# Experts on the chosen tokens alone: routing lists on chip, gathered rows, one-hot sums

## The chip, the cores and the metric

The kernel runs on one core of a Trainium2 chip. The metric is the device time in microseconds (us). A core has TensorE (PE, matrix products), VectorE (DVE), ScalarE (ACT), GpSimd (POOL) and SyncE (SP); each runs its own list of instructions in order, and they wait for each other through semaphores. TensorE first loads a stationary matrix (shown apart, as PEld) and then streams the moving one. Results of TensorE lie in PSUM, eight banks of 128 x 512 f32; everything else lies in SBUF, of 128 partitions.

## The reference

The input is x, 2 batches of 1024 tokens of 128 numbers. Four layers are added to it one after the other, each on a layer norm of x: attention A (16 heads, rotary part), the expert layer, attention B, and the same expert layer again. The case is about the expert layer:

```python
capacity = max(1, int(Sz * CAP_FACTOR / E) + 1)        # 257 for 1024 tokens, 8 experts
scores = softmax(einsum('bsd,ed->bse', x, router_w))
gate_vals, sel_idx = top_k(swapaxes(scores, 1, 2), capacity)
tokens = x[b_idx, sel_idx]                             # (2, 8, 257, 128)
h = gelu(einsum('becd,edh->bech', tokens, w1) + b1)    # 128 -> 512
y = einsum('bech,ehd->becd', h, w2) + b2               # 512 -> 128
out = zeros_like(x).at[b_idx, sel_idx].add(y * gate_vals[..., None])
```

Each expert takes the 257 tokens of a batch that score highest for it. A token can be taken by several experts, or by none.

## The kernel before

The program runs the stages attention A, expert layer 1 (`k` = 0), attention B, expert layer 2 (`k` = 1). Between two stages all engines meet (`nc.Block`). An expert layer is `feed_forward_stage` (L1207). The change leaves the attention stages alone, but for where one of their buffers is allocated.

**Head of the stage.** The tokens are in four chunks of 512. Of each chunk `turn` (L1305) turns the normalised rows by TensorE, so that the 128 numbers of a token lie in the partitions; ScalarE copies them from PSUM twice, as the rounded high part `xr[0]` (L1410) and as `xt` in full (L1411); VectorE makes the low part `xr[1]`, what the rounding left (`split`, L1456). `logits` (L1313) are products of `xt` and the router. Short products without use (`keep_busy`, L417) stand between these steps. After the last logits VectorE and ScalarE make the softmax (L1514 to L1519).

**Main loop.** The experts run over all tokens, not over the chosen ones: 8 experts x 4 chunks = 32 rounds `q`. `hidden` (L1344) is four groups of three products with 512 moving columns (high x high, high x low, low x high part); ScalarE applies the gelu (L1437) and rounds the result (L1443), VectorE makes its low part (`low`, L1461). `output` (L1357) is again twelve such products, one round later. So a round has 24 products of 512 columns, a stage 768. `gate` (L1466) multiplies the output by the gate, which is zero where the token wasn't chosen, and adds it up; at the end `turn_sum` (L1338) turns the four sums back and `finish` (L1488) adds them to x.

**Routing inside the loop.** Which tokens are chosen is found by a search for the 257th largest score of each expert, bit by bit, 30 steps (`step`, L1534): VectorE counts the scores at or above a trial value (L1526), one small product adds the counts over the tiles (L1328), VectorE sets the bit. These steps stand at fixed places (`FIRST_COUNT`, `COUNT_EVERY`) between the groups of products of the first rounds. Nothing in the products depends on them: the first three experts' outputs are kept (`ykeep`, L1446) and gated after the search. The gates go to DRAM and come back spread over the partitions, by SP's queue (L1266). The weights of an expert come through the same queue, two experts ahead (L1257).

**What sets the order.** `vector_events`, `load_events` and `routing` write out by hand at which place (`u`) of the loop each small step stands; TensorE, ScalarE and VectorE follow that list.

Of the kernel before, what the change touches and what calls it, by code (L numbers as in the profile page):

```python
# [13 lines left out]
ALU = mybir.AluOpType  # L14
# [7 lines left out]
P = 128  # L22
# [118 lines left out]
KEEP = 3  # L141
CHUNKS = NE * NCH
BITS = range(29, -1, -1)
SCORE_TURN, FIRST_COUNT, COUNT_EVERY = 4, 6, 3
TIES = FIRST_COUNT + len(BITS) * COUNT_EVERY
NGS = 8


def unit_of(q):

    return 8 * q - 4 if q else 0


def beside_step(u):

    return u + (FIRST_COUNT - u) % COUNT_EVERY if u < TIES else u


def vector_events():

    events = []
    for q in range(CHUNKS):
        events.append((beside_step(unit_of(q) + 5), 1, "low", (q, 0, 2)))
        events.append((beside_step(unit_of(q) + 8) if q else 8, 1, "low", (q, 2, 4)))
        if q >= KEEP * NCH:
            events.append((unit_of(q) + 17, 2, "gate", q))
        else:
            events.append((unit_of(q + KEEP * NCH + 3) + 11, 3, "gate", q))
        if q >= CHUNKS - NCH:
            events.append((unit_of(q) + 24, 4, "finish", q - CHUNKS + NCH))  # L170
    for i in range(len(BITS)):
        events.append((FIRST_COUNT + i * COUNT_EVERY, 0, "step", i))
    events.append((TIES, 0, "ties", 0))
    return sorted(events, key=lambda event: event[0:2])


def load_events():

    events = [(0, 0, "first", 0), (0, 1, "second", 0), (0, 2, "first", 1), (0, 3, "second", 1), (TIES, 4, "gates", 0)]
    for e in range(2, NE):  # L180
        events.append((unit_of((e - 1) * NCH) - 3, 5, "first", e))
        events.append((TIES if e == KEEP + 1 else unit_of((e - 1) * NCH) + 14, 6, "second", e))
    at = [u for u, _, what, q in EVENTS if what == "gate"]
    for n in range(CHUNKS):
        events.append((TIES if n < NGS else at[n - NGS] + 1, 7, "spread", n))
    return sorted(events, key=lambda event: event[0:2])


EVENTS = vector_events()
GATED = [q for _, _, what, q in EVENTS if what == "gate"]  # L190
LOADS = load_events()
LOWS = [q for _, _, what, q in EVENTS if what == "low"]
LOW_DONE = {(q, first): n + 1 for n, (q, first, end) in enumerate(LOWS)}

# [65 lines left out]
def constants(nc, ctx, m, a):  # L260
# [4 lines left out]
    with ExitStack() as local:  # L265
# [4 lines left out]
        b2 = sb("b2_rows", [NE, D], F32)  # L270
        small = local.enter_context(nc.psum_tensor("c_turn", [P, CH], F32))
        with nc.Block() as block:

            @block.sync
            def _(sp):
# [8 lines left out]
                sp.wait_ge(loaded, 16 * (NCH + 4))  # L284
# [28 lines left out]
            @block.tensor  # L313
            def _(pe):
                pe.wait_ge(loaded, 16 * (NCH + 4))
                pe.wait_ge(made, 6)
                pe.transpose(small[:, 0:NE], rw[:, :], m.ident[0:NE, 0:NE]).then_inc(turned, 1)
                pe.transpose(small[:, P:P + NE * HB], b1[:, :], m.ident[0:NE * HB, 0:NE * HB]).then_inc(turned, 1)
                pe.transpose(small[:, 2 * P:2 * P + NE], b2[:, :], m.ident[0:NE, 0:NE]).then_inc(turned, 1)

            @block.vector
            def _(dve):
                dve.wait_ge(loaded, 16 * (NCH + 4))
                dve.tensor_copy(m.peers[:, :, :], peers[:, :, :])
                dve.wait_ge(turned, 3)
# [87 lines left out]
IDLE = {"project": {"a": 0, "b": 36}, "attend": {"a": 34, "b": 10}, "piece": 2, "sum": 8, "turn": [(0, 0, 10, 0), (4, 4, 22, 0)],  # L413
# [754 lines left out]
def project_and_attend(nc, ctx, m, a, kind, norm):  # L1168

    loaded = [ctx.enter_context(nc.semaphore(f"loaded_{kind}{i}")) for i in range(NBUF if kind == "a" else WAYS)]  # L1170
    with ExitStack() as local:
        sb = lambda name, shape, dt: local.enter_context(nc.sbuf_tensor(f"{kind}_{name}", shape, dt))
        shape, count = ([P, GH, T], NBUF) if kind == "a" else ([P, GH // 2, T], WAYS)
        m.q2, m.k2 = [[sb(f"{side}2_{i}", shape, F32R) for i in range(count)] for side in "qk"]
# [4 lines left out]
        with nc.Block() as block:  # L1179
# [27 lines left out]
def feed_forward_stage(nc, ctx, m, a, k, sb, banks, out, norm):  # L1207

    sem = lambda name: ctx.enter_context(nc.semaphore(f"f{k}_{name}"))
# [5 lines left out]
    turned, x_taken, x_split = sem("turned"), sem("x_taken"), sem("x_split")  # L1215
    logits_ready, exp_done, scored = sem("logits_ready"), sem("exp_done"), sem("scored")
    rows_turned, count_ready, total_ready = sem("rows_turned"), sem("count_ready"), sem("total_ready")
    h_mm, gelu_done, h_high, h_low = sem("h_mm"), sem("gelu_done"), sem("h_high"), sem("h_low")
    y_mm, kept, gated = sem("y_mm"), sem("kept"), sem("gated")
    gates_out, sum_ready, sum_turned, finished = sem("gates_out"), sem("sum_ready"), sem("sum_turned"), sem("finished")  # L1220

    peak, e_x, total, score = sb("peak", [P, NT]), sb("e", [P, NT, NE]), sb("total", [P, NT]), sb("score", [P, NT, NE])
    rows = sb("rows", [P, P])
    trial, drop = sb("trial", [P, 1], I32), sb("drop", [P, 1], I32)
    above, count, totals = sb("above", [P, P]), sb("count", [P, 2], BF16), sb("totals", [P, 2])
    tied, rank, need, take = sb("tied", [P, P]), sb("rank", [P, P]), sb("need", [P, 1]), sb("take", [P, P])
    gate_rows = sb("gate_rows", [P, P])
    xr = [sb(f"xr_{i}", [P, B * T], F32R) for i in range(2)]
    w1r, w2r = [[sb(f"w{w}r_{i}", [P, 2, HID], F32R) for i in range(2)] for w in (1, 2)]
    h = [sb(f"h_{i}", [P, HB, CH]) for i in range(2)]  # L1230
    hr = [[sb(f"hr_{i}_{j}", [P, HB, CH], F32R) for j in range(2)] for i in range(2)]
    ykeep = sb("ykeep", [P, KEEP * NCH, CH])
    scaled = [sb(f"scaled_{i}", [P, CH]) for i in range(2)]
    total_t = m.xn[:, :, :].rearrange("p t d -> p (t d)")
    spread = [t[:, i * CH:(i + 1) * CH] for t in (m.v[:, :, :].rearrange("p t d -> p (t d)"), m.xt[:, :]) for i in range(NCH)]

    h_ps, y_ps = banks[:, 0:HB, :], banks[:, HB:HB + 2, :]
# [3 lines left out]
    t_ps = [banks[:, 6 + c % 2, :] for c in range(NCH)]
    use = {q: n for n, q in enumerate(GATED)}
    weights_in = lambda e: 16 * (k * NE // 2 + e // 2 + 1)
    gates_in = lambda n: 16 * (k * CHUNKS // 2 + n // 2 + 1)
# [445 lines left out]
```

## Time and profile before

| | us |
|---|---|
| three runs: lowest, median, highest | 1047.78, 1048.47, 1049.33 |
| profiled execution: span, first to last instruction | 1043.1 |
| median minus that span | 5.4 |
| expert layer 1: first expert product to end of stage | 349.8 to 539.5 |
| expert layer 2: first expert product to last work of TensorE and VectorE | 853.7 to 1040.4 |
| TensorE, VectorE, ScalarE busy of the span | 91%, 71%, 66% |
| granted TensorE clock, mean | 0.981 |

The page gives the span of the profiled execution, and no time of its own beside it; the 5.4 us are what lies before and after. The page reads as follows: part 1 is busy time by engine, part 2 the span in 40 slices (with the granted TensorE clock and the DMA share), part 4 the chain of waits from the last instruction back, part 5 the costliest groups. In a group, "128x512 f32 x768 | 191.4, 397" means 768 instructions that write 128 partitions by 512 numbers, 191.4 us busy in all, 397 ns each; "128\*128" ahead of it is the size of the stationary matrix. Matmuls overlap, so the distance from start to start, not the duration of one, says how fast they go.

### The profile page before, as it was taken

What the parts mean: (1) busy time and instruction counts of PE and PEld (TensorE: products, weight loads), DVE (VectorE), ACT (ScalarE), POOL (GpSimd) and SP (SyncE); (2) the same over time, 40 slices, a digit from 0 to 9 for tenths busy, and PEclk for the clock granted to TensorE, in tenths of its full rate; (3) what the DMA queues carried; (4) which work ended last, traced back from release to release, by engine and by line L of the source; (5) the groups of instructions that cost most, each with busy time, mean ns of one, the idle gap of its engine ahead of it and who ended that gap; (6) DMA issues with size and microseconds to landing.
All of it is one profiled execution on the core that took longest, in us unless ns stands there. A gap on an engine that the chain in (4) does not pass through costs nothing. (4 is left out here: it accounts for less than half of the span.)

```text
span 1043.1 us, 16038 instructions
## 1 busy us (share of the span) xinstructions
PE 950.8 (91%) x5690; PEld 617.5 (59%) x5690; DVE 743.1 (71%) x1318; ACT 691.1 (66%) x1180; POOL 219.0 (21%) x494
## 2 busy tenths in 40 slices
PE   3879999999998899999987899999999889999997
PEld 2545555665655677888764344444444367778886
DVE  4786776677644667699875877777777457678996
ACT  2425666666665698888734356666666759898885
POOL 1352355563333000000005113222332200000000
PEclk9999999999999899999999699999999999999999
DMA  3752442213111011355505360111000021115542
GB/s 91 208 174 41 145 115 74 56 63 91 63 42 45 38 41 41 88 136 141 121 3 131 81 184 1 32 32 32 2 2 1 2 81 41 41 62 125 141 150 51
DMA packets 67727, 78.52 MB, mean 75 GB/s; under 512 B 6512, under 2 KB 55552, under 8 KB 67264
## 3 DMA queue, kind: packets, MB, share of 16 engines
q1 hardware_dynamic: 62432, 72.83, 25.2%
q10 hardware_dynamic: 5216, 4.66, 1.6%
q8 instruction: 46, 0.75, 0.3%
q14 instruction: 33, 0.27, 0.1%
HBM read 53.44 MB, written 22.94 MB: 73 GB/s over the span
## 5 line engine op out<-in xcount | busy, mean ns | idle before, releaser
L1062 ACT ACTIVATE b_pt<-b_banks 128x512 f32<-128x512 f32 (+1 forms) x320 | 154.8, 558 | 99.1 <-PE b_banks L976 98.9
L1369 PE MATMUL f_banks<-f_hr,f_w2r 128*128 128x512 f32 x768 | 189.1, 394 | 3.6 <-DVE f_hr L1463 2.5
L1353 PE MATMUL f_banks<-f_xr,f_w1r 128*128 128x512 f32 x768 | 191.4, 397 | 0.7 <-ACT f_h L1437 0.7
L1437 ACT ACTIVATE f_h<-f_banks,b_t 128x512 f32<-128x512 f32 x256 | 167.2, 682 | 32.3 <-PE f_banks L1353 29.8
L1463 DVE TENSOR_TENSOR f_hr<-f_h,f_hr 128x1024 fp32r<-128x1024 f32 x128 | 156.1, 1223 | 28.1 <-ACT f_hr L1443 26.1
L1369 PEld LDWEIGHTS f_banks<-f_hr,f_w2r 128*128 128x128 f32 x768 | 141.7, 188 | 32.3 <-issue 3.4
L1353 PEld LDWEIGHTS f_banks<-f_xr,f_w1r 128*128 128x128 f32 x768 | 143.3, 191 | 29.6 <-ACT f_h L1437 1.5
L1085 DVE TENSOR_REDUCE a_mlate<-a_banks 128x2 f32<-128x1024 f32 (+3 forms) x120 | 124.7, 1079 | 49.8 <-PE a_banks L914 31.1
L1085 DVE TENSOR_REDUCE b_mlate<-b_banks 128x2 f32<-128x1024 f32 (+3 forms) x120 | 125.7, 1080 | 36.1 <-PE b_banks L924 18.0
L1443 ACT ACTIVATE f_hr<-f_h 128x1024 fp32r<-128x1024 f32 x128 | 136.0, 1063 | 4.1
L1062 ACT ACTIVATE a_q_hl<-a_banks 128x512 f32<-128x512 f32 (+1 forms) x160 | 81.8, 557 | 65.0 <-PE a_banks L976 63.5
L976 PE MATMUL a_banks<-a_q,a_k 121*128 121x512 f32 (+3 forms) x384 | 117.1, 383 | 3.6 <-DMA a_q<-a_mt 2.6
L1062 ACT ACTIVATE a_k_hl<-a_banks 128x512 f32<-128x512 f32 (+1 forms) x160 | 82.2, 557 | 53.4 <-PE a_banks L976 51.8
L914 PE MATMUL a_banks<-a_k,a_q 120*128 120x512 f32 (+3 forms) x384 | 99.2, 361 | 11.3 <-DVE a_mlate L1085 7.7
L976 PE MATMUL b_banks<-b_q,b_k 64*128 64x512 f32 (+3 forms) x384 | 99.0, 421 | 10.5 <-ACT b_pt L1062 8.7
L976 PEld LDWEIGHTS b_banks<-b_q,b_k 64*128 64x128 f32 x384 | 47.9, 190 | 85.4 <-ACT b_pt L1062 55.3
L976 PEld LDWEIGHTS a_banks<-a_q,a_k 121*128 121x128 f32 x384 | 65.1, 190 | 48.5 <-issue 20.1
L914 PE MATMUL b_banks<-b_k,b_q 63*128 63x512 f32 (+3 forms) x384 | 75.7, 384 | 9.9 <-DVE b_mlate L1085 5.8
L994 PE MATMUL b_banks<-b_pt,vg 128*32 128x512 f32 (+3 forms) x768 | 80.8, 511 | 0.0
L914 PEld LDWEIGHTS a_banks<-a_k,a_q 120*128 120x128 f32 x384 | 64.0, 191 | 27.6 <-DVE a_mlate L1085 17.3
L1085 DVE TENSOR_REDUCE b_mearly<-b_banks 128x2 f32<-128x768 f32 (+3 forms) x56 | 49.7, 918 | 23.6 <-PE b_banks L924 22.9
L840 POOL TENSOR_SCALAR_AFFINE_SELECT b_pt<-b_pt 128x128 f32<-128x128 f32 x128 | 36.9, 293 | 134.0 <-ACT b_pt L1062 133.9
(202 smaller groups left out, 1036.5 us busy)
## 6 DMA issues: line engine op xcount, KB each, us to landing
scratch_w<-a_tab SPq DMA_DIRECT2D x16, 512.0 KB, 3.1
f_w1r<-scratch_w SPq DMA_DIRECT2D x16, 512.0 KB, 5.8
f_w2r<-scratch_w SPq DMA_DIRECT2D x16, 512.0 KB, 6.1
v<-scratch_gate SPq DMA_DIRECT2D x32, 256.0 KB, 5.4
xt<-scratch_gate SPq DMA_DIRECT2D x32, 256.0 KB, 5.2
a_rot<-in_w SPq DMA_DIRECT2D x16, 256.0 KB, 4.0
a_q<-scratch_q SPq DMA_DIRECT2D x8, 384.0 KB
a_k<-scratch_k SPq DMA_DIRECT2D x8, 384.0 KB
```

What stands on the lines that cost most here:

```text
L840: pool.affine_select(out=block[:, 0:P], in_=block[:, 0:P], compare_op=ALU.is_ge, fill=0.0, base=0, pattern=[[1, P]], channel_multiplier=-1 ...
L914: last = pe.matmul(to[:, bank, col:col + w], head_rows(q2, n, h, slice(q * P, (q + 1) * P), 0), head_rows(k2, n, h, slice(k0, k0 + w), 0), ...
L976: last = pe.matmul(st[u % NST][:, col:col + w], head_rows(k2, n, h, slice(key * P, (key + 1) * P), 1), head_rows(q2, n, h, slice(c * CH + ...
L994: last = pe.matmul(o_ps[VW * h:VW * (h + 1), q0:CH], vg[n % 2][:, key, h, :], pt[(SET0[i] + s) % NPT][:, h, col:col + w], start=(key == 0) ...
L1062: act.activation(pt[at % NPT][:, h, 0:cols], st[u % NST][:, 0:cols], ACT.Exp, scale=scale).then_inc(exp_done, 1)
L1085: last = dve.tensor_reduce(dst, src, AX.X, ALU.max, negate=True)
L1353: last = pe.matmul(h_ps[:, j, :], w1r[e % 2][:, wp, j * P:(j + 1) * P], xr[xp][:, chunk(c)], start=(i == 0), stop=(i == 2))
L1369: last = pe.matmul(y_ps[:, q % 2, :], w2r[e % 2][:, wp, j * P:(j + 1) * P], hr[q % 2][hp][:, j, :], start=(j == 0 and i == 0), stop=(j == ...
L1437: act.activation(h[q % 2][:, j, :], h_ps[:, j, :], ACT.Gelu, bias=m.b1_t[:, e * HB + j:e * HB + j + 1]).then_inc(gelu_done, 1)
L1443: act.activation(hr[q % 2][0][:, j - 1:j + 1, :], h[q % 2][:, j - 1:j + 1, :], ACT.Copy).then_inc(h_high, 1)
L1463: dve.tensor_tensor(hr[q % 2][1][:, first:end, :], h[q % 2][:, first:end, :], hr[q % 2][0][:, first:end, :].bitcast(F32), ALU.subtract).th ...
```

## The change

The experts now run on the chosen tokens alone. A unit `n` is one batch and one expert, 16 in a stage; its 257 tokens are padded to 258 columns (`WIDE`): 2 blocks (`BLK`) of 128 slots, one left-over token and one column of padding.

- The normalised rows go to DRAM (`store_rows`), and beside each row its 8 scores.
- The search is done for one batch at a time with 16 trial values at once: 8 steps (`SHIFTS`), each a count over 128 x 1024 scores, one per pair of trial value and expert. For this the scores are repeated 16 times and turned (`repeat_scores`, `take_scores`).
- `counts`, `take` and `lists` rank the chosen tokens; `small_out`, `find` and `indices` turn the ranks into a list of row numbers.
- GpSimd fetches the 128 rows of each block by index (`indirect_dma_start`), six units ahead at most (`NXG`); an extra fetch per batch takes the left-over tokens.
- Per unit TensorE turns the fetched rows (`tokens`), does 12 + 12 products of 258 columns, turns the output back (`turn_back`), and adds it to the sums of the batch (`add`): for each of 2 blocks, 8 tiles and 2 parts one product of 128 columns whose stationary matrix is a one-hot matrix (`hot`), made by VectorE from the slot numbers that came back from DRAM (`one_hot`, `spread_place`).
- The routing of batch 0 stands ahead of the loop. That of batch 1 is put into iterations 0 to 5 of the loop (`spot`). The 30-step search, the gates over all tokens, `ykeep`, the low part of all of x and the last `keep_busy` are gone.
- All 8 experts' weights stay in SBUF from the start of the stage. Small tables are added to the constants. The semaphores of both expert layers are the same ones now, cleared by GpSimd at the start of attention B.

The core of the diff (names of the new code; unchanged helpers left out):

```diff
-KEEP = 3
-CHUNKS = NE * NCH
-BITS = range(29, -1, -1)
-SCORE_TURN, FIRST_COUNT, COUNT_EVERY = 4, 6, 3
+SLOTS = CAPACITY - 1
+BLK = SLOTS // P
+WIDE = CAPACITY + 1
+SHIFTS = (26, 22, 18, 14, 10, 6, 2, 0)
+UNITS = B * NE
+NXG, NPOS = 6, 3
+PHASES = [(SEARCH, s) for s in range(len(SHIFTS))] + [(COUNTS, 0), (TAKE, 0), (LISTS, 0), (SMALL, 0), (INDEX, 0)]
+VECTOR_AT = {2 * n - 2: PHASES[n] for n in range(1, len(PHASES))}
+TENSOR_AT = {2 * n - 1: PHASES[n] for n in range(1, TOTALS)}
...
+            for i in range(BLK):
+                pool.indirect_dma_start(token[n % NXG][:, i, :], None, m.scratch["rows"],
+                                        by_row(index[b][:, i, e:e + 1])).then_inc(token_in[n % NXG], 16)
...
+                narrow(b, s - 1)
+                link(dve.tensor_tensor(limit[:, :], m.steps[:, 1:2] if s == 1 else ahead[:, :], drop[:, :], ALU.bitwise_or))
+            link(dve.tensor_scalar(above_all[:, :], rows[:, :], trial.bitcast(F32), 0.0, ALU.is_ge, ALU.add, accum_out=passed[:, :]))
+            dve.tensor_scalar(enough[:, :], passed[:, :], CAPACITY - 0.5, None, ALU.is_ge).then_inc(count_ready, 1)
...
+        def one_hot(n):
...
+            for i in range(BLK):
+                last = dve.tensor_scalar(hot[n % 2][:, i, :], spread[n % NPOS][:, :], m.slot[:, i:i + 1], None, ALU.is_equal)
...
+        def output(n):
...
+            if n:
+                pe.wait_ge(y_low, n)
...
+        def add(n):
...
+            pe.wait_ge(hot_ready, n + 1)
+            pe.wait_ge(y_low, n + 1)
+            for i in range(BLK):
+                for t in range(QT):
+                    for part in range(2):
+                        last = pe.matmul(sum_ps[:, t // TPC, t % TPC * P:(t % TPC + 1) * P], hot[n % 2][:, i, t * P:(t + 1) * P],
+                                         yr[n % 2][:, part, i, :], start=(n % NE == 0 and i == 0 and part == 0 and t % TPC == 0),
+                                         stop=False, skip_group_check=True)
...
+        repeat_scores(0)
+        for what, s in PHASES[:TOTALS]:
+            route(0, what, s)
+        for q in range(4):
+            find(0, q)
+        repeat_scores(1)
+        route(1, *PHASES[0])
+        tokens(0)
+        for i in range(UNITS + 2):
+            for j in range(HB):
+                if i < UNITS:
+                    hidden(i, j)
+                if j == 1:
+                    if 0 <= i - 2:
+                        turn_back(i - 2)
...
+            if i + 1 < UNITS:
+                tokens(i + 1)
+            spot(4 * i + 1)
+            if 0 <= i - 1 < UNITS:
+                output(i - 1)
+            spot(4 * i + 2)
+            if 0 <= i - 2:
+                add(i - 2)
...
+            spot(4 * i + 3)
```

In the loop VectorE's order in iteration i is `one_hot(i-2)`, a routing step, `split_output(i-2)`, `split_tokens(i+1)`, a routing step, `split_hidden(i)`; ScalarE's is two gelus, `split_output(i-2)`, two gelus, `split_tokens(i+1)`, `split_hidden(i)`, `copy_output(i-1)`.

## Rows read from the trace of the kernel before

**Rows 1.** Page, part 1: busy us, share of the span, number of instructions.
```profile
PE 950.8 (91%) x5690; PEld 617.5 (59%) x5690; DVE 743.1 (71%) x1318; ACT 691.1 (66%) x1180; POOL 219.0 (21%) x494
```

**Rows 2.** Windows of both expert loops: length, busy us by engine, clock, DMA share, GB/s.
```profile
349.79:539.50 189.71, 185.38 (x835) 147.01 (x834) 144.62 (x266) 157.19 (x206) 0.00 (x0) 0.99 0.31 79
853.66:1040.40 186.74, 181.78 (x819) 143.78 (x818) 144.66 (x266) 157.17 (x206) 0.00 (x0) 1.00 0.30 84
```

**Rows 3.** Groups by form, TensorE: products and weight loads of the experts.
```profile
L1353 PE MATMUL f_banks<-f_xr,f_w1r 128*128 128x512 f32 x768 | 191.4, 397 | 0.7 <-ACT f_h L1437 0.7
L1353 PEld LDWEIGHTS f_banks<-f_xr,f_w1r 128*128 128x128 f32 x768 | 143.3, 191 | 29.6 <-ACT f_h L1437 1.5
```

**Rows 4.** Timeline, TensorE: start us, us, engine, line, what, how many merged.
```profile
147.96 0.74 PE L914 MATMUL a_banks<-a_k,a_q 120*128 120x256 f32 x4
339.53 0.97 PEld L1316 LDWEIGHTS f_banks<-rw_t,xt 128*128 128x128 f32 x8
```

**Rows 5.** Timeline of layer 1: from the last logits through the softmax.
```profile
348.30 1.71 PE L1316 MATMUL f_banks<-rw_t,xt 128*128 128x8 f32 x8
351.65 0.29 DVE L1519 TENSOR_TENSOR f_score<-f_e,f_total 128x128 f32<-128x128 f32 x1
```

**Rows 6.** Timeline: one step of the search on VectorE, and its product.
```profile
363.03 0.18 PE L1328 MATMUL f_banks<-f_count,peers 128*128 128x1 bf16 x1
363.26 0.16 DVE L1538 TENSOR_SCALAR f_drop<-f_banks 128x1 int32<-128x1 f32 x1 [0.33 <-PE f_banks L1328]
...
363.65 0.35 DVE L1526 TENSOR_SCALAR_CACHE_REDUCE f_above<-f_rows,f_trial 128x128 f32<-128x128 f32 x1
363.92 0.09 DVE L1526 DVE_READ_ACCUMULATOR f_above<-f_rows,f_trial 128x1 bf16 x1
```

**Rows 7.** Groups by form, VectorE.
```profile
L1463 DVE TENSOR_TENSOR f_hr<-f_h,f_hr 128x1024 fp32r<-128x1024 f32 x128 | 156.1, 1223 | 28.1 <-ACT f_hr L1443 26.1
...
L1482 DVE TENSOR_TENSOR xn<-xn,f_scaled 128x512 f32<-128x512 f32 x56 | 38.7, 692 | 1.9
L1477 DVE SCALAR_TENSOR_TENSOR f_scaled<-f_ykeep,b_t,xt 128x512 f32<-128x512 f32 x12 | 9.0, 750 | 0.3
L1139 DVE CAST a_k<-a_k 96x1024 fp32r<-96x1024 f32 x1 | 0.7, 690 | 1.3 <-DMA a_k<-a_q 1.3
L1555 DVE TENSOR_SCALAR f_rank<-f_rank,f_need 128x128 f32<-128x128 f32 x2 | 0.6, 288 | 0.1
L1558 DVE TENSOR_TENSOR f_gate_rows<-f_rows,f_take 128x128 f32<-128x128 f32 x2 | 0.6, 293 | 0.1
```

**Rows 8.** Groups by form, ScalarE.
```profile
L1437 ACT ACTIVATE f_h<-f_banks,b_t 128x512 f32<-128x512 f32 x256 | 167.2, 682 | 32.3 <-PE f_banks L1353 29.8
L1062 ACT ACTIVATE b_pt<-b_banks 128x512 f32<-128x512 f32 x256 | 134.1, 601 | 80.4 <-PE b_banks L976 80.2
L1062 ACT ACTIVATE b_pt<-b_banks 128x256 f32<-128x256 f32 x64 | 20.7, 389 | 18.7 <-PE b_banks L976 18.6
L365 ACT ACTIVATE xn<-x,sc 128x128 f32<-128x128 f32 x32 | 13.1, 482 | 7.5 <-DVE sc L357 7.5
```

**Rows 9.** DMA issues: what, queue, how many, KB each, median us to landing.
```profile
f_w1r<-scratch_w SPq DMA_DIRECT2D x16, 512.0 KB, 5.8
...
out<-x SPq DMA_DIRECT2D x4, 256.0 KB, 2.3
```

**Rows 10.** Windows around and at the lower clock.
```profile
576.50:583.30 6.80, 5.09 (x30) 2.21 (x28) 6.80 (x8) 3.22 (x5) 1.17 (x4) 1.00 0.39 121
347.80:354.60 6.80, 6.80 (x23) 5.73 (x23) 2.10 (x6) 3.84 (x6) 0.00 (x0) 0.50 0.00 0
583.34:603.82 20.48, 18.16 (x85) 8.53 (x83) 14.35 (x17) 6.75 (x14) 2.76 (x8) 0.50 0.36 83
```

**Rows 11.** Timeline of the constants: the last load's issue, and VectorE's first work.
```profile
4.48 0.32 SPq L283 DMA_DIRECT2D b_rows<-in_b  x1
10.65 0.29 DVE L324 CAST peers<-peers_f 128x256 bf16<-128x256 f32 x1 [10.65 <-DMA b_rows<-in_b]
```

More of the change, by code:

```diff
@@ L177, in load_events @@
[L177 to L186, printed above, removed]
@@ L189, with table_columns @@
[L189 to L193, printed above, removed]
+SLOTS = CAPACITY - 1
+BLK = SLOTS // P
+WIDE = CAPACITY + 1
+ROW = D + NE
+TE = QT * NE
+WAYS16 = P // NE
+SHIFTS = (26, 22, 18, 14, 10, 6, 2, 0)
+HUGE = 1 << 30
+UNITS = B * NE
+NXG, NPOS = 6, 3
+TABLE = {}
+def table_columns():
+    at = 0
+    for name, width in (("iota", WIDE), ("gmask", NE), ("tile_of", B * NE), ("left_of", B), ("slot", BLK), ("half", BLK),
+                        ("last", 1), ("same", P)):
+        TABLE[name] = slice(at, at + width)
+        at += width
+    return at
@@ L1224, in feed_forward_stage @@
[L1224 to L1237, printed above, removed]
+    many_ready = sem("many_ready")
+    above_all, own = sb("above_all", [P, T], BF16), sb("own", [TE, P])
@@ new lines, in feed_forward_stage @@
+    drop, base, ahead, limit = (sb(n, [P, 1], I32) for n in ("drop", "base", "ahead", "limit"))
+    passed, enough = sb("passed", [P, 1]), sb("enough", [P, 1], BF16)
+    above, tied, rank, take_, run = (sb(n, [TE, P]) for n in ("above", "tied", "rank", "take", "run"))
+    count, totals, need, in_tile = sb("count", [TE, 2], BF16), sb("totals", [TE, 2]), sb("need", [TE, 1]), sb("in_tile", [TE, 1], BF16)
+    first, end = sb("first", [TE, 1]), sb("end", [TE, 1])
+    past, holds, slot_of = sb("past", [TE, WIDE]), sb("holds", [TE, WIDE], BF16), sb("slot_of", [TE, P], BF16)
@@ L1241, in feed_forward_stage @@
[L1241 to L1244, printed above, removed]
+    l_ps = banks[:, 6, 0:P]
     chunk = lambda c: slice(c * CH, (c + 1) * CH)
@@ L1499, in vector @@
             chunk_norm_vector(dve, m, norm, 3)
-            for c in order:
-                split(c)
         else:
@@ L1507, in vector @@
             chunk_norm_vector(dve, m, norm, 2)
-            for c in order:
-                split(c)
         dve.wait_ge(logits_ready, NCH)
@@ L1560, in vector @@
[L1560 to L1571 removed]
+        dve.wait_ge(scored, 2)
+        repeat_scores(0)
+        for what, s in PHASES:
+            phase(0, what, s)
+        repeat_scores(1)
+        phase(1, *PHASES[0])
@@ L1573, in feed_forward_stage @@
+        finish(1)
     stage = Stage()
```

702 lines of the change are left out of this document (470 added, 232 removed).

## The prediction

> **What bounds the kernel now.** I read the page's busy shares first: TensorE is busy 91% of the span, VectorE 71%, ScalarE 66% [rows 1]. A busy TensorE is not yet one at its peak, so the windows of the two expert loops come next: 185.4 of 189.7 us and 181.8 of 186.7 us busy, VectorE at 145 and ScalarE at 157 us in each [rows 2]. The groups by form say what fills them: 768 + 768 products of 512 columns in both layers [rows 3], so 768 a loop; 189.7 / 768 gives 0.247 us each with all else, and 512 columns at 2.4 GHz are 0.213. The loops are bound by TensorE's moving columns: 376 of 1043 us. The change cuts the columns of a loop from 768 x 512 to 384 x 258. Two things set against that: products that are bound by their weights, and a routing that nothing covers.
>
> The page gives the span, 1043.1 us; the median of the runs is 5.4 more. I add up changes of the span and put the 5.4 on top.
>
> **Prices.** Weights: eight products that move only 8 columns load their f32 weights in 0.97 us [rows 4]; less the last one's 0.19 [rows 3], over 7 steps, that is 0.111 us a load. The count of loads equals that of products, 768 [rows 3], although two of every three share their weights: none is saved. Four products of 256 columns take 0.74 us [rows 4]; less 0.28 for the last and 0.107 for the first load, over 3: 0.118 us each. So 258 columns cost 0.118, and 128 columns or fewer 0.111, the load.
> VectorE: 128x512 without a pointer is 0.692, with one 0.750 [rows 7]: the pointer costs 0.055. The count over 128 numbers takes 0.35 [rows 6] = 0.293 [L1558, rows 7] + 0.055, one number a cycle; over 1024 numbers it is 0.35 + 896/0.96 GHz = 1.28. TENSOR_SCALAR with a pointer takes 0.288 over 128 [L1555, rows 7], 0.055 less, and a cast of 1024 numbers 0.69 [rows 7]: two numbers a cycle. So a one-hot block is 0.69 + 0.055, two of them 1.4 back to back. Small operations are 0.16 with 0.04 between [rows 6].
> ScalarE: 0.60 and 0.39 for 512 and 256 columns, so 0.21 less for 258; a gelu 0.682 - 0.21 = 0.47, or 0.36 from start to start; with a pointer scale about 0.38 for 128 columns [rows 8].
>
> **Removed.** Both loops: 189.7 and 186.7 us. In the head one of two copies and the wait for the low part: about 1.1 a layer (two 0.6 us copies per chunk [rows 8] become one).
>
> **Added ahead of the loop, per layer, on the path.** After the last logits (348.30 + 1.71 = 350.0) the scores are there at 351.94 [rows 5]: 2.1. Repeating the scores: copy 0.7, eight turns and a wait 0.7, two ScalarE copies and a small one 1.4: 2.9. Search: a step is two small operations (0.4), the count (1.28 + 0.09), the comparison (0.2): 1.95 to the count's signal; then product and hand-over 0.18 + 0.1 + 0.1 [rows 6]: 2.35. Eight steps, the first without narrowing: 18.4. `counts` 1.75, `take` 2.3, `lists` 3.0 (of which 1.2 for 64x1024), `small_out` 1.5, `find` and `indices` 4.5 (four ScalarE operations of 512 at 0.5, then a reduction of 1024 at 1.22): 13.05. Fetch by index: no row has a DMA of GpSimd. From below: SP issues in 0.32 [rows 11] and 256 KB land in 2.3 [rows 9], so 3; from above two of the slowest loads in a row, 2 x 5.8 [rows 9] = 12. I take 5.6, nearer the small transfer since 128 rows are 70 KB. Turning and splitting the first tokens 1.9. Sum 44.0 from the last logits. Weights (8 MB) land beside it.
>
> **The loop, per layer.** TensorE's work in a unit: 24 x 0.118 = 2.83, one-hot products 32 x 0.111 = 3.55, six short ones 0.67: 7.05. On top comes a wait in every iteration: `output(i-1)` waits for `y_low(i-2)`. The turn-back ends 0.93 after the iteration's start, ScalarE finishes it after the second gelu at 2.1 (2 x 0.38), VectorE needs 0.6 more: 2.8. TensorE has finished hidden and tokens at 2.1. So 0.75 idle, iteration 7.8; iterations 6 to 15: 78. VectorE (1.4 + 0.65 + 0.4 + 1.22 = 3.7) and ScalarE (about 4) aren't the bound there.
> Iterations 0 to 5 carry batch 1's routing, and TensorE waits in order for each of its steps. Iteration 2: VectorE is still 1.3 behind, one-hot to 2.7, step to its signal 4.7, end 5.1, low part of the output 5.8; then TensorE does output 1.4 and add 3.55, takes step two 0.3: 11.2. By the same rule iterations 0 to 5 take 5.0, 6.3, 11.2, 8.6, 8.5 and 10.3: 49.9, where TensorE alone has 35.
> Change of batch: 16 products of the left-over tokens 1.8, its waits and `finish(0)` on VectorE 1.5: 3.3. Tail: iteration 16 is turn, split, output, add 6.8; iteration 17 split 2.3, add 3.55, left-over 1.8, `finish` 1.6: 16.0. Loop: 147.2.
>
> **Clock.** TensorE idles during the 42 us of routing and waits 15 us in iterations 0 to 5. Before it fell to 0.50 of the clock (1.2 GHz) for 20.5 us it had been busy 5.1 of 6.8 us, and it stayed there while busy 18.2 of 20.5 [rows 10]. A lower clock doubles what lies on the path there. From below 0, from above output and add of four iterations, 4 x 5, less clock 20; I take 3 a layer, as another stretch of before lasted 6.8 us [rows 10].
>
> **Sum.** Layer 1: 44.0 + 147.2 - 1.1 - 189.7 = +0.4. Layer 2: 190.1 - 186.7 = +3.4. Clock +6. Constants: two more loads and eight small copies beside what now ends a wait at 10.65 [rows 11]: +1.6. The last store is 512 instead of 256 KB behind `finish`: +0.9. Together +12.3: span 1055.4, time 1060.8, say 1061. SP's queue: the stores of rows and scores stand between weight loads that land in 5.8 us [rows 9], done before 400; the list's store waits for nothing late. GpSimd's queue holds only the fetches: the first of batch 1 waits for its list, and three units of batch 0 are then long fetched.
>
> **Rules of the skill.** The trace reads two numbers a cycle for TENSOR_SCALAR and one for the count. The Trainium skill, VectorE: DVE Perf Modes, section The perf-mode tier table, gives fp32 tensor_scalar in SBUF 2x without an exception for the count. By that rule the count is 0.75: rival C.
> No row shows a fetch by GpSimd beside VectorE. The Trainium skill, SBUF — State Buffer, section SBUF: two separate sides, says that GpSimd can't write descriptors while VectorE runs a two-port operation. It speaks against this change, whose one-hot blocks would be such; rival D.
>
> **Rivals.**
> A, the other side: TensorE is not held by the routing and the wait for `y_low`. If VectorE's steps fit beside the products, iterations 0 to 5 fall to 40 (35 plus start), and half of the wait of 0.75 goes: per layer -9.9 - 3.8, and no clock loss, -3: -16.7. It decides if TensorE idles under 15 us in the loop. 1061 - 33 = 1028. For: sums of single steps by full latency run high, the windows of before show TensorE idle only 4 to 5 us. Against: four hand-overs lie in series in each iteration.
> B, clock: half clock through iterations 0 to 5: +17 a layer over my 3: 1095. For: the 20.5 us at 0.50 [rows 10]. Against: the mean granted clock of the loops was 0.99 and 1.00 [rows 2].
> C, the count at two numbers a cycle: 8 x 0.53 exposed and 6 x 0.53 in the loop, 7.4 a layer: 1046. Against: 0.346 fits one a cycle.
> D, the fetch late, 12 us instead of 5.6: +6.4 a layer, 1074. It decides only at the loop's start; afterwards two fetches have 7.8 us and six buffers.
> E, the change does not do what it says (products that depend on the data): the sizes are constants, so I give it nothing.
>
> **Chances.** Forecast 0.43 (own range 1046 to 1078), A 0.28, B 0.12, C 0.09, D 0.08. What can be told from no change is 0.2%, 2.1 us: 1046.4 to 1050.6. Faster: 0.27 of A, 0.04 of the forecast's low end, 0.04 of C: 0.35. Same: 0.03 of the forecast, 0.01 of A, 0.03 of C: 0.07. Slower 0.58. Range for 8 in 10: from 1018, which takes in A and a little below it, to 1100 with most of B.
>
> **What would show it.** Right: from the last logits to the first expert product 44 us, 18 of them the eight counts at 1.28; count operations of 1.28, one-hot blocks of 0.75; one-hot products with start to start 0.111; iterations 6 to 15 at 7.8 with TensorE idle before the output products on VectorE; iterations 0 to 5 at 50. Wrong: count operations at 0.75; the first token rows over 10 us after the list; clock 0.50 past iteration 5; one-hot products under 0.08 or over 0.2, which would move a layer by 16 us or more.

## The result, and the profile after

| | before | changed |
|---|---|---|
| runs, us | 1047.8, 1048.5, 1049.3, 1051.8 | 1072.0, 1079.8, 1083.8, 1088.3 |
| median, us | 1048.9 | 1081.8 |
| profiled execution: span, us | 1043.1 | 1070.2 |
| granted TensorE clock in it, mean | 0.981 | 0.916 |

The ratio of the changed kernel to the one before is 1.030, 95% interval 1.024 to 1.036: slower. A run more than 1.5% above the fastest of its kernel (1088.3 here, and two of the four of e9 below) counts in the medians and not in the ratios. The profiled run of the changed kernel is its fastest, 1.8 us over its span. The others (clock 0.905, 0.904 and 0.893) are 8 to 16 us longer: the time goes with the clock.

The changed kernel's page, part 1 and the clock of part 2. TensorE is busy 68 us less [rows 1], in a longer span, and two valleys of low clock (slices 14 to 16 and 33 to 35) stand where the routing of batch 0 is:

```profile
PE 882.5 (82%) x6204; PEld 603.0 (56%) x6204; DVE 676.5 (63%) x1338; ACT 517.5 (48%) x1084; POOL 293.6 (27%) x562
PEclk9999999999999557998979799999999975799997
```

Windows of the changed kernel, columns as in [rows 2]. In each layer, four stretches: from the last logits to the first expert product, iterations 0 to 5, 6 to 15, and from iteration 16 to the last sum (the tail).

```profile
350.30:394.20 43.90, 10.15 (x42) 6.11 (x43) 30.38 (x97) 6.40 (x13) 5.84 (x6) 0.50 0.53 179
394.20:448.98 54.78, 45.96 (x310) 42.23 (x311) 40.90 (x107) 25.39 (x54) 11.75 (x13) 0.84 0.15 35
448.98:533.30 84.32, 79.56 (x635) 76.59 (x635) 38.20 (x66) 38.59 (x90) 19.90 (x17) 0.96 0.17 43
533.31:552.34 19.03, 14.54 (x99) 13.73 (x98) 4.07 (x9) 1.96 (x6) 0.00 (x0) 0.80 0.00 1
...
866.07:909.54 43.47, 9.91 (x43) 5.87 (x43) 30.56 (x97) 6.41 (x13) 5.72 (x6) 0.53 0.54 188
909.54:963.68 54.14, 44.31 (x310) 40.57 (x311) 40.98 (x107) 25.25 (x54) 10.69 (x13) 0.87 0.15 36
963.68:1046.48 82.80, 78.02 (x635) 75.24 (x635) 38.21 (x66) 38.59 (x90) 19.90 (x17) 0.98 0.20 50
1046.48:1066.59 20.11, 15.62 (x99) 14.81 (x98) 4.07 (x9) 1.96 (x6) 0.00 (x0) 0.76 0.00 1
```

From the last logits a layer takes 202.0 and 200.5 us here, where the loops of [rows 2] took 189.7 and 186.7. The routing in the open eats what the shorter loop (158.1 and 157.0) saves, and more.

Groups by form, expert layer 1. The one-hot products are the largest group of the loop, and their weight loads are busy as long as they are. The last figures of a row are TensorE's idle time before the group: ahead of the output products (L1474) it is 6.0 us in the whole layer.

```profile
L1498 PE MATMUL f_banks<-f_yr,f_hot 128*128 128x128 f32 x512 | 60.5, 277 | 1.8 <-DVE f_yr L1808 1.8
L1498 PEld LDWEIGHTS f_banks<-f_yr,f_hot 128*128 128x128 f32 x512 | 59.9, 195 | 2.3 <-issue 2.3
...
L1461 PE MATMUL f_banks<-f_xr,f_wr 128*128 128x258 f32 x192 | 35.1, 327 | 3.4 <-ACT f_h L1585 1.3 <-issue 1.1 <-DVE f_xr L1793 1.0
L1474 PE MATMUL f_banks<-f_hr,f_wr 128*128 128x258 f32 x192 | 30.2, 312 | 6.0 <-DVE f_yr L1808 5.8
...
L1787 DVE TENSOR_SCALAR f_hot<-f_spread,slot 128x1024 fp32r<-128x1024 bf16 x32 | 22.6, 748 | 0.0
...
L1676 DVE TENSOR_SCALAR_CACHE_REDUCE f_above_all<-xn,f_limit 128x1024 bf16<-128x1024 f32 x14 | 17.9, 1279 | 0.5
```

One search step, timeline, answering to [rows 6]. Counts start at 357.93 and 360.15: 2.22 us a step, seven times in a row.

```profile
357.93 1.28 DVE L1676 TENSOR_SCALAR_CACHE_REDUCE f_above_all<-xn,f_limit 128x1024 bf16<-128x1024 f32 x1
...
359.26 0.16 DVE L1677 TENSOR_SCALAR f_enough<-f_passed 128x1 bf16<-128x1 f32 x1
...
359.47 0.19 PE L1402 MATMUL f_banks<-f_enough,same 128*128 128x1 bf16 x1 [1.96 <-DVE f_enough L1677]
...
359.77 0.16 DVE L1688 TENSOR_SCALAR f_drop<-f_banks 128x1 int32<-128x1 f32 x1
359.96 0.16 DVE L1674 TENSOR_TENSOR f_limit<-f_ahead,f_drop 128x1 int32<-128x1 int32 x1
360.15 1.28 DVE L1676 TENSOR_SCALAR_CACHE_REDUCE f_above_all<-xn,f_limit 128x1024 bf16<-128x1024 f32 x1
```

One thing in the trace no step of the prediction had. Leaving out 9 and 10, where the batch changes (20.8 us together in layer 1, 19.3 in layer 2), iterations 6 to 15 run at 7.71 to 7.75 us, but iteration 7 takes 9.39 in layer 1 and 9.41 in layer 2. Timeline of its start, TensorE, ScalarE, and GpSimd:

```profile
456.73 0.93 PE L1461 MATMUL f_banks<-f_xr,f_wr 128*128 128x258 f32 x6
...
459.01 0.84 ACT L1585 ACTIVATE f_h<-f_banks,b_t 128x258 f32<-128x258 f32 x2 [5.13 <-PE f_banks L1461]
...
459.54 0.39 PE L1461 MATMUL f_banks<-f_xr,f_wr 128*128 128x258 f32 x1 [1.31 <-ACT f_h L1585]
...
455.31 1.02 POOL L1350 DMA_INDIRECT f_token<-scratch_rows,f_index  x1 [0.30 <-issue]
456.63 0.95 POOL L1350 DMA_INDIRECT f_token<-scratch_rows,f_index  x1 [0.30 <-issue]
```

The three products of the first gelu end at 457.30 and ScalarE has been free for 3.4 us; it starts at 459.01, 1.71 us late. I call this a late start: the first instruction after a wait begins over 0.4 us behind the end of its last input. Looking at every gelu and every split of tokens on ScalarE, the trace has six, 0.9 to 1.8 us each, all in iterations 0, 1 and 7. GpSimd issues 13 fetches without a break from 386.8 to 404.0 and seven from 448.7 to 457.6. In all six the last input comes in such a burst (or in layer 2's) or within 1.2 us behind it; the work itself begins up to 2.4 us behind the burst's last issue.

### The profile page after: what moved, and what is told of

It is laid out like the page before. It is cut to its first block and busy times, and to the rows that moved or that the text cites. A ratio compares the mean times of both kernels' runs of the same rounds, so it can differ in the third digit from the quotient of the medians.

```text
span 1070.2 us, 16736 instructions
## 1 busy us (share of the span) xinstructions
PE 882.5 (82%) x6204; PEld 603.0 (56%) x6204; DVE 676.5 (63%) x1338; ACT 517.5 (48%) x1084; POOL 293.6 (27%) x562
## 5 line engine op out<-in xcount | busy, mean ns | idle before, releaser
L1498 PE MATMUL f_banks<-f_yr,f_hot 128*128 128x128 f32 x1024 | 121.8, 278 | 3.6 <-DVE f_yr L1808 3.6
L1498 PEld LDWEIGHTS f_banks<-f_yr,f_hot 128*128 128x128 f32 x1024 | 120.6, 197 | 4.6 <-issue 4.6
L1585 ACT ACTIVATE f_h<-f_banks,b_t 128x258 f32<-128x258 f32 x128 | 55.4, 481 | 112.6 <-PE f_banks L1461 111.2
L1350 POOL DMA_INDIRECT f_token<-scratch_rows,f_index x64 | 69.3, 1083 | 108.5 <-DVE f_yr L1808 93.2
L981 PEld LDWEIGHTS a_banks<-a_q,a_k 121*128 121x128 f32 x384 | 65.0, 190 | 48.6 <-issue 20.3
L1461 PE MATMUL f_banks<-f_xr,f_wr 128*128 128x258 f32 x384 | 69.9, 327 | 6.3 <-ACT f_h L1585 3.1
L1474 PE MATMUL f_banks<-f_hr,f_wr 128*128 128x258 f32 x384 | 58.7, 306 | 11.9 <-DVE f_yr L1808 11.6
L1808 DVE SCALAR_TENSOR_TENSOR f_yr<-f_banks,f_token,f_yr 128x128 fp32r<-128x128 f32 x64 | 19.5, 347 | 76.4 <-ACT f_yr L1606 58.3
```

The costliest lines, as they stand in the source:

```text
L981: last = pe.matmul(st[u % NST][:, col:col + w], head_rows(k2, n, h, slice(key * P, (key + 1) * P), 1), head_rows(q2, n, h, slice(c * CH + ...
L1350: pool.indirect_dma_start(token[n % NXG][:, i, :], None, m.scratch["rows"], by_row(index[b][:, i, e:e + 1])).then_inc(token_in[n % NXG], 16)
L1461: last = pe.matmul(h_ps(n, j), wr[:, e, 0, wp, j * P:(j + 1) * P], xr[n % 2][:, xp, :], start=(i == 0), stop=(i == 2))
L1474: last = pe.matmul(y_ps, wr[:, e, 1, wp, j * P:(j + 1) * P], hr[n % 2][hp][:, j, :], start=(j == 0 and i == 0), stop=(j == HB - 1 and i == 2))
L1498: last = pe.matmul(sum_ps[:, t // TPC, t % TPC * P:(t % TPC + 1) * P], hot[n % 2][:, i, t * P:(t + 1) * P], yr[n % 2][:, part, i, :], star ...
L1585: act.activation(h[n % 2][:, j, :], h_ps(n, j), ACT.Gelu, bias=m.b1_t[:, e * HB + j:e * HB + j + 1]).then_inc(gelu_done, 1)
```

## The experiments

Twelve kernels ran; each ratio is to the kernel before on the same chip. The theory after the result: TensorE's order and its weight loads set the iteration, the loop's first six iterations are held by batch 1's routing, and the missing time is low clock and late starts.

**Operands exchanged (e1).** TensorE's products for the sums, and a copy, turn and addition at each batch's end:

```diff
-            for i in range(BLK):
-                for t in range(QT):
-                    for part in range(2):
-                        last = pe.matmul(sum_ps[:, t // TPC, t % TPC * P:(t % TPC + 1) * P], hot[n % 2][:, i, t * P:(t + 1) * P],
-                                         yr[n % 2][:, part, i, :],
+            for half in range(2):
+                for i in range(BLK):
+                    for part in range(2):
+                        last = pe.matmul(sum_ps[:, half, :], yr[n % 2][:, part, i, :], hot[n % 2][:, i, half * CH:(half + 1) * CH],
...
```

> Sums of a unit with the operands exchanged: the weighted output is stationary, the one-hot matrix moves 512 columns, 8 products a unit instead of 32, and 4 instead of 16 for the left-over tokens; the sums of a batch are copied, turned and joined to x at its end. Theory (TensorE's order and its weight loads set the iteration): 8 products of 512 columns at about 0.22 us take 1.8 us where 32 took 3.4; iterations 6 to 15 go from 7.75 to about 6.1 us, iterations 0 to 5 lose less because they are held by the routing (about 1 us each), the tail gains 3 us and pays 1.5 us for the turning: about -24 us a layer, span near 1022, ratio to the kernel before 0.98. Rival (VectorE or the hand-overs are the bound, products only fill their waits): iterations stay above 7 us, gain under 8 us a layer.

Median 1018.3, ratio 0.972 (0.966 to 0.977). Windows of e1, iterations 0 to 5 and 6 to 15, and its products by form:

```profile
396.10:444.92 48.82, 39.01 (x215) 32.56 (x216) 38.81 (x104) 25.14 (x54) 10.67 (x12) 0.81 0.16 39
444.92:507.73 62.81, 59.15 (x390) 52.52 (x389) 39.85 (x70) 38.51 (x91) 20.80 (x17) 1.00 0.23 57
...
L1509 PE MATMUL f_banks<-f_hot,f_yr 128*128 128x512 f32 x128 | 34.9, 416 | 1.8 <-DVE f_yr L1847 1.8
```

The steady iteration went from 7.73 to 6.0 us, the 1.7 us of the theory (32 products at 0.110 against 8 at 0.23 from start to start). Both forms move 4096 columns a unit. The same sums with a quarter of the weight loads made the kernel faster than the one before: with products bound by their loads, the shorter loop wasn't short enough.

**Turning back earlier (e2).**

```diff
 for i in range(UNITS + 2):
+    turn_back(i - 2)            # TensorE; split_output(i - 2) likewise on ScalarE
     for j in range(HB):
         hidden(i, j)
-        if j == 1: turn_back(i - 2)
```

> Turning back unit i-2 stands at the head of iteration i, ahead of the hidden products, on TensorE and ScalarE; nothing else changes. Theory (every iteration loses 0.65 us because the output products wait for the low part of unit i-2): the wait before the output products goes, iterations 6 to 15 go from 7.75 to 7.1 us, about -7 us a layer, span near 1056. Rival (the gelu, now 0.6 us later, holds the hidden products through their three banks instead): iteration unchanged within 0.2 us, span 1066 or more.

Median 1082.9, ratio 1.035 (1.031 to 1.040), no better than the changed kernel. The rival holds. Timeline of a steady iteration of e2, TensorE:

```profile
505.76 1.96 PE L1461 MATMUL f_banks<-f_xr,f_wr 128*128 128x258 f32 x12
507.56 0.38 PE L1447 MATMUL f_banks<-ident,f_token 128*128 128x128 f32 x2
...
508.18 1.73 PE L1474 MATMUL f_banks<-f_hr,f_wr 128*128 128x258 f32 x12
509.75 3.69 PE L1498 MATMUL f_banks<-f_yr,f_hot 128*128 128x128 f32 x32
```

The wait ahead of L1474 is gone, but it was small: in a steady iteration of the changed kernel TensorE idles 0.26 us there (504.78 to 505.04), not the 0.65 of this expectation or the 0.75 of the prediction. The hidden products take 0.138 us from start to start in the first six and 0.173 in the last six, instead of 0.131 and 0.137; the tenth starts 0.05 us behind the end of the first gelu, for whose bank it waits. The iteration is 7.65 us, 0.09 less.

**Filling for the clock (e3, e6, e12).** e3 puts 12 to 22 small products ahead of each routing step of batch 0 and 50 behind the list:

```diff
+            keep_busy(pe, m, banks[:, 5, 0:2 * P], FILL[what])     # 15 ahead of a search step
             route(0, what, s)
...
+        keep_busy(pe, m, banks[:, 5, 0:2 * P], 50)
         repeat_scores(1)
```

> Small bf16 products (256 columns) fill TensorE's waits during batch 0's routing and the first fetch, nothing else changes. Theory (the clock fell because TensorE idled there, and iterations 0 to 2 pay for it): granted clock 1.00 from the last logits into iteration 2, iterations 0 to 2 go from 27.7 to about 23 us, the routing before the loop gains at most 1 us: about -5 us a layer, span near 1060. Rival 1 (iterations 0 to 2 are held by the routing of batch 1 on VectorE, not by the clock): less than 1.5 us a layer. Rival 2 (the extra work is paid back in a lower clock later in the layer): span equal or longer than 1070, low clock moved behind iteration 2.

Median 1087.2, ratio 1.041 (1.036 to 1.046). The clock was 1.00 from 353 to 394 us in layer 1, and the way to the first expert product got 1.1 us shorter. Then it fell to 0.50 for 17 us, through most of iterations 0 and 1, so the theory's full clock into iteration 2 didn't come about: in layer 1 iterations 0 to 2 took 31.7 us. And the 50 products stand ahead of `repeat_scores(1)`, which VectorE waits for; in layer 2, in part at half clock, they pushed the first expert product 4.5 us back. Late starts came too, the longest at 3.8 us: iteration 0 took 13.1 us. Timeline of e3, ScalarE in iteration 0:

```profile
396.87 0.48 ACT L1590 ACTIVATE f_h<-f_banks,b_t 128x258 f32<-128x258 f32 x1 [2.30 <-remote]
399.00 0.48 ACT L1590 ACTIVATE f_h<-f_banks,b_t 128x258 f32<-128x258 f32 x1 [1.65 <-remote]
403.23 0.39 ACT L1583 ACTIVATE f_xr<-f_banks 128x258 fp32r<-128x258 f32 x1 [3.75 <-remote]
```

e6 moved the filling: none ahead of `repeat_scores(1)`, 24 ahead of the first tokens, 12 in each of iterations 0, 1, 16 and 17.

> Small bf16 products keep TensorE busy in its waits once more, but placed so that none stands ahead of a step that something waits for: in the routing of batch 0, ahead of the first tokens, in iterations 0 and 1, and 12 each in iterations 16 and 17. Theory (clock): granted clock 1.00 from the routing into iteration 2 and in the tail; the first expert product 1 us earlier, iterations 0 to 2 about 3 us shorter, the tail 3 us shorter: -7 us a layer, span near 1056. Rival 1 (VectorE's steps and late hand-overs hold iterations 0 to 2): only the tail's 3 us a layer, span near 1064. Rival 2 (the filling is paid back by a lower clock behind it): span 1070 or more.

Median 1084.8, ratio 1.038 (1.032 to 1.044). The tail went from 19.0 and 20.1 to 17.1 and 16.2 us, as expected. But iterations 0 to 5 took 59.8 and 60.9 us with late starts of up to 3.7, and the 24 products ran at 0.2 us each at the lower clock: the first expert product came 2.3 us later in layer 1 and 4.1 in layer 2. The span, 1081.2, is that of rival 2.

e12 adds the filling without those 24 to the paced kernel e5 below:

> The changed kernel with the fetches paced and TensorE's waits filled (in the routing of batch 0, 12 small products in each of iterations 0, 1, 16 and 17; none ahead of the first tokens). Without the late starts this reads what the low clock costs the changed kernel, against the paced one (median 1064.5, iterations 0 to 5 of 54.8 and 50.7 us, from iteration 16 to the last sum joined 20.2 and 21.4 us). Theory (the low clock costs mainly the tail): from iteration 16 to the end 16.5 us, iterations 0 to 5 about 49 us, routing 42.8 us: -6 to -8 us a layer, median near 1051. Rival (the filling moves the low clock to other work on the path): median 1060 or more.

Median 1065.0, ratio 1.019 (1.015 to 1.024); e5 has 1.017. The rival holds. Windows of e12: the tails of the two layers.

```profile
533.97:550.90 16.93, 15.06 (x123) 14.00 (x122) 4.07 (x9) 1.96 (x6) 0.00 (x0) 0.91 0.00 1
1041.70:1057.87 16.17, 14.31 (x123) 13.29 (x122) 4.07 (x9) 1.96 (x6) 0.00 (x0) 0.96 0.00 0
```

The tail is 3.3 and 5.3 us shorter than in e5 (20.2 and 21.4), but iterations 0 to 5 are 3.0 and 2.3 us longer (57.8 and 53.0 against 54.8 and 50.7), most of it in iterations 0 and 1, where I read that twelve small products at half clock are longer than the wait that they fill. In layer 1 the clock also fell in iterations 5 and 6 (0.90 and 0.76, 1.00 in e5), and iteration 6 took 9.39 instead of 7.73 us. The medians show no gain.

**Count twice in batch 1 (e4).**

```diff
             link(dve.tensor_scalar(above_all[:, :], rows[:, :], trial.bitcast(F32), 0.0, ALU.is_ge, ALU.add, accum_out=passed[:, :]))
+            if b == 1:
+                link(dve.tensor_scalar(above_all[:, :], rows[:, :], trial.bitcast(F32), 0.0, ALU.is_ge, ALU.add, accum_out=passed[:, :]))
```

> The count over 1024 scores is made twice in each search step of batch 1 only (the steps inside iterations 0 to 3). Theory (TensorE waits in order for each of batch 1's steps): each of the 7 doubled counts in the loop adds its 1.3 us, less about 2 us of cover: +7 us a layer, span near 1084. Rival (the routing of batch 1 fits beside the products): under +2 us a layer.

Median 1101.6, ratio 1.055 (1.049 to 1.060). Window of e4, iterations 0 to 5 of layer 1:

```profile
393.13:457.27 64.14, 49.54 (x311) 46.00 (x311) 50.11 (x121) 25.76 (x54) 11.96 (x14) 0.77 0.12 31
```

Iterations 0 to 5 took 64.1 and 63.0 us instead of 54.8 and 54.1: 9.4 and 8.8 more. The seven added counts stand in iterations 0 to 3, which took 7.8 and 8.8 us more for 9.2 us of counts (1.32 each); 1.6 us of layer 1 are iteration 5 at a clock of 0.86. So most of an added count is in the open, with 0.4 to 1.4 us of cover where I had given 2, and the rival falls. How much of this is a lower clock (0.77 against 0.84) and other late starts is not separated, and the rest of the difference in the medians isn't broken down.

**Fetches paced (e5), and without an index (e9).**

```diff
 # e5, GpSimd
+            if n >= 2:
+                pool.wait_ge(x_low, n - 1)
 # e9, GpSimd, no pacing
-                pool.indirect_dma_start(token[n % NXG][:, i, :], None, m.scratch["rows"], by_row(index[b][:, i, e:e + 1]))
+                pool.dma_start(token[n % NXG][:, i, :], m.scratch["rows"][b * T + i * P:b * T + (i + 1) * P, :])
```

> GpSimd fetches the rows of unit n (n of 2 or more) only when the rows of unit n-2 are split, so the bursts of 13 and 7 fetches at the start of each batch become one pair an iteration. In the trace of the changed kernel ScalarE starts 0.9 to 1.8 us late in iterations 0, 1 and 7 with its operands ready, and each of these times lies in or just behind a burst of fetches. Theory (the bursts cause it): the late starts go, iteration 7 returns from 9.4 to 7.75 us, iterations 0 and 1 lose about 2 us together: -3.5 us a layer, span near 1063. Rival (they have another cause and only fall into the same stretch): late starts stay, span 1070 or more.

Median 1064.5, ratio 1.017 (1.009 to 1.025). No late start is left on ScalarE, iteration 7 takes 7.73 and 7.74 us, iterations 0 and 1 together 12.9 and 13.1 instead of 15.8 and 16.6. With iteration 7 that is 4.6 and 5.1 us a layer. In layer 2 iterations 0 to 5 fell from 54.1 to 50.7. In layer 1 they stayed at 54.8: iterations 2 and 3 ran at a clock of 0.75 and 0.81 and took 3.0 us more. Groups of up to five issues by index back to back are left in e5, without a late start. Windows of e5, iterations 6 to 15 of layer 1 (the changed kernel has 84.32 in the row above):

```profile
447.30:528.46 81.16, 77.83 (x636) 75.23 (x635) 38.21 (x66) 38.52 (x90) 16.82 (x17) 0.98 0.18 44
```

> The changed kernel with 256 and more of its token fetches made without an index: GpSimd issues the same number of transfers, at the same points and of the same size, but of 128 fixed consecutive rows (so the list is made and not used, and the output is left wrong). Theory (the issue of a transfer by index, 0.95 us of GpSimd each, is what delays the other engines' hand-overs): no late start on ScalarE, iteration 7 at 7.75, iterations 0 and 1 near 13 us together, the first tokens turned 1 to 3 us earlier after the list is ready, -5 us a layer or more, median near 1070. Rival 1 (the traffic of the bursts delays them, whoever names the rows): late starts as before, only the first fetch shorter. Rival 2 (nothing in the fetch matters, pacing worked by chance): median 1080 and late starts.

Median 1073.9, ratio 1.016 (1.010 to 1.022), near the paced kernel's, but from two runs only (1058.0 and 1070.0); the profile is of a run of 1077.9. No late start either, iterations 0 and 1 at 13.5 us, iteration 7 at 7.74, although the twelve fetches still went out back to back. The six first iterations took 56.6 and 56.5 us, with iteration 2 at a clock of 0.66 and 0.65. Timeline of GpSimd, e9 and then the changed kernel:

```profile
390.36 2.74 POOL L1351 DMA_DIRECT2D f_token<-scratch_rows  x5
```

```profile
388.21 0.97 POOL L1350 DMA_INDIRECT f_token<-scratch_rows,f_index  x1 [0.31 <-issue]
389.49 0.94 POOL L1350 DMA_INDIRECT f_token<-scratch_rows,f_index  x1 [0.30 <-issue]
```

Transfers of the same size at 0.55 us an issue do no harm, those by index (0.95 us each, 1.26 from start to start) do. But the plain burst is also shorter: in layer 1 it ends 0.7 us into iteration 0, and that of batch 1 3.5 us ahead of iteration 7, while the indexed ones reach into iterations 1 and 7. So e5 shows that the late starts come with long bursts of issues by index; whether the index or the length and place of the burst counts, e9 doesn't separate. The first tokens were turned 5.8 us after the list instead of 6.2, so most of the fetch's latency is not the index's. What it is in such a burst that holds ScalarE is not shown.

**Put together (e7, e8, e10, e11).** e7 is exchanged operands and pacing; e8 adds e6's filling; e10 is e8 without the 24 products ahead of the first tokens; e11 moves a step:

```diff
 # e11, VectorE; on TensorE output(i - 1) is put ahead of spot(4 * i + 1) likewise
-            spot(4 * i)
             if 0 <= i - 2:
                 split_output(i - 2)
+            spot(4 * i)
```

> Operands of the sums exchanged and the fetches paced. Theory: the two gains add up, median near 1011 (1018 less 3.5 a layer). Rival (late starts not from the bursts): the median stays at 1018.

Median 1009.5, ratio 0.966 (0.959 to 0.972): the gains add, 8.8 us off e1's median, with no late start left.

> Operands of the sums exchanged, fetches paced, and TensorE's waits filled as in the kernel that fills alone. Theory: gains add, median near 1000. Rival (clock and bursts are worth nothing): 1018 or more.

Median 1006.7, ratio 0.962 (0.957 to 0.968), not told apart from e7: iterations 0 to 5 are 2.2 and 1.4 us shorter, the first product 1.9 us later.

> Operands exchanged, fetches paced, waits filled, but without the 24 filling products ahead of the first tokens, which ended 2.3 us too late. Theory: first expert product 43 us after the last logits instead of 45.7, the rest as before: -2.7 us a layer, median near 1001. Rival (without them TensorE starts at half clock, and iterations 0 and 1 give it back): 1006.

Median 1007.3, ratio 0.961 (0.958 to 0.963). The rival: the first product came after 42.7 us instead of 45.8, and iteration 0 took 7.6 and 7.3 instead of 5.9 us at a lower clock.

> The same, and in iterations 0 to 5 the low part of the output and the output products stand ahead of a step of batch 1's routing, on VectorE and on TensorE. Theory (in these iterations one-hot, routing step and low part lie in series ahead of the output products): about 1 us less in each of four iterations, -4 us a layer, median near 993. Rival (the step is only moved and the second step of the iteration ends as late): iterations 0 to 5 unchanged, no gain.

Median 1011.0, ratio 0.965 (0.962 to 0.967): no better than e10, and the theory falls. Iteration 2 shrank from 10.4 (11.4 in layer 2) to 7.6 us, but iteration 1 went from 7.2 (5.8 in layer 2) to 8.6 and iteration 5 from 9.6 to 12.1 and 12.5; the six took 52.0 instead of 48.6 and 47.8. All five kernels with exchanged operands beat both kernels; e7, e8, e10 and e11 by 3.4 to 3.9% against the one before.

## Why the prediction was right, and where it was off

Forecast: slower, 1061 (span 1055.4, 12.3 more than before). Measured: slower, 1081.8 at the median (33 more), span 1070.2 in the fastest run (27.1 more). The mechanism given is the measured one: routing in the open against a loop shortened less than its columns. The size was less than half, short by 14.8 us of span: the two loops are 14.7 over, and the other terms nearly cancel. The direction had some luck. In the sum, routing and loop came within 0.4 and 3.4 us a layer of the loop that they replace; half of the 12.3 us was the clock, whose 3 us a layer were chosen between 0 and 20. What the sum missed lay on the slower side.

| step | predicted | layer 1, layer 2 |
|---|---|---|
| last logits to first expert product | 44.0 | 43.9, 43.5 |
| count over 1024; search step | 1.28; 2.35 | 1.28; 2.22 |
| list ready to first tokens turned | 5.6 | 6.2, 5.9 |
| one-hot product, start to start; one-hot block | 0.111; 0.745 | 0.110; 0.748 (both layers) |
| steady iteration | 7.8 | 7.71 to 7.75 |
| iterations 0 to 5 | 49.9 | 54.8, 54.1 |
| iterations 6 to 15 with the change of batch | 81.3 | 84.3, 82.8 |
| tail | 16.0 | 19.0, 20.1 |
| loop with 3 us for the clock | 150.2 | 158.1, 157.0 |

- **Weights.** The 0.111 us from eight tiny products [rows 4] were right to 1%, and e1 shows that they decide. The 0.118 for 258 columns holds as well: most steps from one hidden product to the next are 0.115 to 0.126. The prediction had the price and not the remedy.
- **Routing.** Sums of single steps by their full latency came out within 0.5 us over 44, in part because their errors cancel: in layer 1 the search took 17.5 us for 18.4 and the way from its end to the list 12.5 for 13.05, but repeating the scores took 3.6 for 2.9 and the fetch 6.2 for 5.6. By the tier table of the Trainium skill (VectorE: DVE Perf Modes, The perf-mode tier table) the count would take 0.75, by the prediction's estimate; it took 1.28, one number a cycle. The measurement decides, and rival C falls.
- **Steady iteration.** 7.74 for 7.8 is in part luck as well: the idle time ahead of the output products is 0.26 us and not 0.75, while these products take 0.129 us from start to start and not 0.118.
- **Rival A** (the loop hides batch 1's routing) falls with e4: an added count costs most of its time. Without late starts, and at full clock from iteration 2 on (0.74 in the first two), iterations 0 to 5 are 50.7 us (e5, layer 2), near the predicted 49.9.
- **The failed size** is the loop's sum, by two terms. First, late starts behind the bursts of indexed fetches: 4.6 and 5.1 us a layer by e5, and I had none; the text on SP's and GpSimd's queue said only that units "are then long fetched", and that very fetching ahead came with the cost. Second, the clock, 3 us a layer in the sum. Less the late starts the loops are still 6.3 and 4.7 us over the 147.2 without a clock term; this is an estimate of what the clock took, with small errors of other terms in it, and no run isolates it. The tail alone lost some 3 to 4 (19.0 and 20.1 against 16.2 at clock 0.96 in e12), and iteration 2 of layer 1 1.35 (11.88 against 10.53). It is not rival B: the clock was 0.84 and 0.87 in iterations 0 to 5, not half.
- **Rival D**, the late fetch, fell: 6.2 us. Its rule is visible in part: eight issues of 1.8 to 1.9 us instead of 0.95 stand where VectorE begins its one-hot blocks. The Trainium skill (SBUF — State Buffer, SBUF: two separate sides) says that GpSimd can't write descriptors during such an operation. The trace agrees for these eight; six other issues beside one-hot blocks took only 0.98 to 1.22, and one of 1.80 has no such block beside it. No late start lies at any of the eight. Timeline of the changed kernel:

```profile
462.53 1.89 POOL L1350 DMA_INDIRECT f_token<-scratch_rows,f_index  x1 [0.30 <-issue]
463.52 1.42 DVE L1787 TENSOR_SCALAR f_hot<-f_spread,slot 128x1024 fp32r<-128x1024 bf16 x2
```

- **Small terms.** The 1.6 us for constants were 0.2. The head gained nothing in layer 1 instead of 1.1: in both kernels the last logits ran at half clock and ended 15.5 us after the first turning of the stage; in layer 2 it gained 0.6. The last store cost its 0.9 (span's end 3.6 us behind the last sum, 2.7 before). Ahead of attention B 36 small products took 6.9 us at the lower clock where they had taken 4.1.
- **The offset.** I put 5.4 us on the span. The changed kernel's profiled run is 1.8 over its span; the rest of the 5.4 is that the profiled run was faster than the median, and from span to median the changed kernel has 11.6.

## What to carry to other kernels

Price a product by its weight load as well as by its columns, and put the operand with more columns on the moving side: the same sums took 1.7 us less an iteration with 8 products of 512 columns than with 32 of 128. Work that replaces covered work has to be covered too: 44 us of routing in the open, with VectorE busy for 30 of them, ate what 384 x 258 instead of 768 x 512 columns saved. Issue fetches by index when they are needed, not in one burst as far ahead as the buffers allow.

## What the runs showed of the hardware that I had not expected

- While GpSimd issued indexed fetches back to back (13 in 17.2 us), ScalarE began work that it had waited for up to 1.8 us late, in the other kernels with such bursts up to 3.8 us (e3). There were none in the seven kernels with paced or plain fetches and some in the six others. Its cause is open.
- TensorE's clock fell to its lower level (0.50, 1.2 GHz) near the last logits of layer 1 for 6.8 us in the kernel before and for 51.2 us in the changed one, through the routing into iteration 0. Small products held it at 1.00 there (e3), and bought 1.1 us, since VectorE's count and not TensorE was on the path; it fell as they ended, at 394.0, for 17 us.
- The changed kernel's four runs spread over 16 us, in the order of their granted clocks. Those of before spread over 4 here and over up to 11 beside the experiments, between 1041.0 at a clock of 0.984 and 1052.0 at 0.973.
